# A feed-forward stage that moves its residual rows by whole groups of four batches instead of by halves

## The reference

```python
x = x + _L0_xattn_ref(_layernorm(x), ctx_1024, ctx_1024, igate_w, igate_b, fgate_w, fgate_b, out_w)
x = x + _L0_ffn_ref(_layernorm(x), L0_ffn_weight)
x = x + _L1_xattn_ref(_layernorm(x), ctx_1024, Wq, Wkv)
x = x + _L1_ffn_ref(_layernorm(x), w_gate, w_up, w_down)

def _bitlinear(x, w):
    return jnp.einsum('bsi,oi->bso', _act_quant(x), _weight_quant(w))
gate = jax.nn.silu(_bitlinear(x, w_gate))
up = _bitlinear(x, w_up)
return _bitlinear(gate * up, w_down)
```

## Time and profile before

| | us |
|---|---|
| median of three executions | 652.21 (652.16 to 652.42) |
| the profiled execution | 652.21 |
| its span, first to last instruction | 649.8 |
| PE busy | 614.1 (94%) |
| DVE busy | 567.8 (87%) |
| ACT busy | 535.9 (82%) |
| POOL busy | 454.8 (70%) |

### The profile page before, as it was taken

One profiled execution on the slowest core, in us unless ns is written; L12 is line 12 of the kernel. 1 busy time (PEld: TensorE's weight loads), 2 busy tenths in 40 slices (PEclk: granted clock), 3 DMA queues, 4 the chain that ended last, 5 costly groups with the idle time before them and its releaser, 6 DMA issues.

```text
span 649.8 us, 14695 instructions
## 1 busy us (share of the span) xinstructions
PE 614.1 (94%) x4562; PEld 456.3 (70%) x4562; DVE 567.8 (87%) x1461; ACT 535.9 (82%) x1298; POOL 454.8 (70%) x676
## 2 busy tenths in 40 slices
PE   5879999999999999999999999999899999999996
PEld 4658687687877878878787687877456556655664
DVE  4787899998898988989889889898999899999994
ACT  4577889889889789897897978965789989989985
POOL 3357586777855868658676586762677888887877
PEclk9999999999999999999999999999999999999999
DMA  8306414163351441424505233024276777686763
GB/s 291 133 8 124 98 34 131 49 146 101 80 131 50 114 106 43 131 55 111 129 18 132 58 106 99 18 66 162 46 134 163 164 167 160 157 182 158 183 124 106
DMA packets 141808, 72.53 MB, mean 112 GB/s; under 512 B 89245, under 2 KB 141470, under 8 KB 141734
## 3 DMA queue, kind: packets, MB, share of 16 engines
q1 hardware_dynamic: 134870, 68.21, 42.5%
q10 hardware_dynamic: 6864, 3.41, 1.7%
HBM read 29.39 MB, written 20.97 MB: 77 GB/s over the span
## 4 chain that ended last, share of the span: by engine, by line
PE 56%; DVE 16%; ACT 16%; issue 4%; POOL 4%; DMA 2%; SPq 1%; POOLq 0%; DVEq 0%; ACTq 0%
PE bank L743 10%; PE bank L658 8%; PE bank L711 8%; PE bank L688 8%; PE bank L762 5%; PE bank L568 4%; PE bank L732 4%; ACT ew L905 4%; PE bank L623 3%; ACT D L896 3%; DVE vg L1635 2%; DVE hmax L1642 2%; ACT x2T L872 2%; PE bank L614 2%; DVE st L1339 2%
## 5 line engine op out<-in xcount | busy, mean ns | idle before, releaser
L743 PE MATMUL bank<-WGU,fqT 128*128 128x512 bf16 x512 | 124.6, 380 | 2.4 <-DVE vg L1635 1.9
L1181 POOL TENSOR_SCALAR_AFFINE_SELECT D<-D 128x512 f32<-128x512 f32 x64 | 38.4, 635 | 85.9 <-ACT D L896 85.9
L1635 DVE SCALAR_TENSOR_TENSOR vg<-bank,back,D 128x1024 f32<-128x1024 f32 x64 | 82.0, 1280 | 7.4 <-ACT D L1076 5.8
L1076 ACT ACTIVATE D<-bank,back 128x1024 f32<-128x1024 f32 x64 | 71.4, 1115 | 18.4 <-PE bank L743 18.2
L743 PEld LDWEIGHTS bank<-WGU,fqT 128*128 128x128 bf16 x512 | 46.8, 98 | 56.4 <-DVE vg L1635 22.3
L1166 POOL TENSOR_TENSOR rs<-ve,minus_half 128x4 f32<-128x4 f32 x64 | 65.6, 1026 | 28.2 <-DVE ve L1345 26.7
L1642 DVE TENSOR_REDUCE hmax<-vg 128x1 f32<-128x1025 f32 x64 | 78.1, 1221 | 2.2
L1289 POOL TENSOR_SCALAR wtmp<-vg,hscale 128x1024 f32<-128x1024 f32 x64 | 71.6, 1119 | 5.9 <-issue 0.2
L1339 DVE BATCH_NORM_STATS2 st<-x 128x6 f32<-128x256 f32 x184 | 64.6, 413 | 2.7
L688 PEld LDWEIGHTS bank<-vaug,C 128*128 128x128 f32 x512 | 60.7, 192 | 2.2 <-issue 1.5
L658 PE MATMUL bank<-WX,qcT 128*128 128x268 f32 x256 | 62.0, 395 | 0.0
(11 more groups left out here) (200 smaller groups left out, 1537.0 us busy)
## 6 DMA issues: line engine op xcount, KB each, us to landing
xg<-in_x_dram SPq DMA_DIRECT2D x16, 512.0 KB, 3.9
cg<-in_ctx_dram SPq DMA_DIRECT2D x16, 512.0 KB, 4.6
out_dram<-x SPq DMA_DIRECT2D x15, 512.0 KB, 3.3
out_dram<-x SPq DMA_DIRECT2D x30, 256.0 KB, 2.3
xg<-out_dram SPq DMA_DIRECT2D x16, 256.0 KB, 2.9
cg<-out_dram SPq DMA_DIRECT2D x16, 256.0 KB, 3.2
rows_q<-fq ACTq DMA_DIRECT2D x13, 256.0 KB, 2.3
raw<-in_L_ffn_w_gate_dram SPq DMA_DIRECT2D x1, 1024.0 KB, 8.1
```

What stands on the lines that cost most here:

```text
L743: mm = pe.matmul(ps[k + half], fqT[:, i // 2 % 2, c, i % 2 * P:(i % 2 + 1) * P], WGU[:, c, which, half * 512:(half + 1) * 512], start=(c = ...
L1076: act.activation(fsil[:, s % 2, :], gate, ACT.Silu, scale=back[:, i, 0:1]).then_inc(g_clear, 1)
L1635: dve.scalar_tensor_tensor(out=fh[i % 2][:, 0:INNER], in0=up, scalar=back[:, i, 1:2], in1=fsil[:, i % 2, :], op0=ALU.mult, op1=ALU.mult).t ...
```

## The change

The halves go. One load of 512 KB, written inline, replaces two of 256 KB, and `half_out` becomes `group_out`: it waits for all four batches, stores them in one transfer and issues the whole load of four groups later. In the loop it moves from the even blocks (two for each group) to every fourth block, i % 4 == 3, from block 11 on. The semaphores `f_in` and `f_out` lose their second index, and POOL waits for them once in a group. Counts at the end follow.

```diff
-        f_in = [[sem(f"f_in{p}_{h}") for h in range(2)] for p in range(4)]
-        f_out = [[sem(f"f_out{p}_{h}") for h in range(2)] for p in range(2)]
+        f_in = [sem(f"f_in{p}") for p in range(4)]
+        f_out = [sem(f"f_out{p}") for p in range(2)]
...
-            def half_in(g, h):
-                some = slice(2 * h, 2 * h + 2)
-                sp.dma_start(fx[g % 4][:, some, :], grp(out, g)[:, some, :]).then_inc(f_in[g % 4][h], 16)
-
             for g in range(4):
-                for h in range(2):
-                    half_in(g, h)
+                sp.dma_start(fx[g], grp(out, g)).then_inc(f_in[g], 16)
             store(NG - 2)
-            def half_out(g, h):
-                some = slice(2 * h, 2 * h + 2)
-                sp.wait_ge(f_done, FB * g + 2 * h + 2)
-                sp.dma_start(grp(out, g)[:, some, :], fo[g % 2][:, some, :]).then_inc(f_out[g % 2][h], 16)
+            def group_out(g):
+                sp.wait_ge(f_done, FB * g + FB)
+                sp.dma_start(grp(out, g), fo[g % 2][:, :, :]).then_inc(f_out[g % 2], 16)
                 if g + 4 < NG:
-                    half_in(g + 4, h)
+                    sp.dma_start(fx[g % 4], grp(out, g + 4)).then_inc(f_in[g % 4], 16)
...
-                if i % 2 == 0 and i >= 2 * FB:
-                    half_out(i // FB - 2, i % FB // 2)
+                if i % FB == 3 and i > 2 * FB:
+                    group_out(i // FB - 2)
...
-            half_out(NG - 2, 0)
-            half_out(NG - 2, 1)
+            group_out(NG - 2)
...
-                if s % 2 == 0:
-                    pool.wait_ge(f_out[g % 2][s // 2], 8 * (g - g % 2) + 16)
-                    pool.wait_ge(f_in[g % 4][s // 2], 4 * (g - g % 4) + 16)
+                if s == 0:
+                    pool.wait_ge(f_out[g % 2], 8 * (g - g % 2) + 16)
+                    pool.wait_ge(f_in[g % 4], 4 * (g - g % 4) + 16)
```

More of the change, by code:

```diff
@@ L514, in _ @@
             for p in range(2):
-                for h in range(2):
-                    sp.wait_ge(f_out[p][h], 8 * NG + 16 - 16 * p)
+                sp.wait_ge(f_out[p], 8 * NG + 16 - 16 * p)
             sp.wait_ge(f_last, 16 * FB)
@@ L1325, in _ @@
             for p in range(2):
-                for h in range(2):
-                    dve.sem_inc(f_out[p][h], 16)
+                dve.sem_inc(f_out[p], 16)
             chain = [0]
```

## The result

| | before | changed |
|---|---|---|
| median | 653.17 us (13 runs, 651.4 to 655.8) | 657.75 us (13 runs, 655.5 to 660.5) |
| ratio | | 1.0060 (1.0042 to 1.0078) |
| profiled execution, span | 652.21, 649.8 | 658.11, 656.3 |
| third silu to last silu of the loop | 636.88 - 459.50 = 177.4 | 643.35 - 461.99 = 181.4 |
| last silu to the end of the span | 12.9 | 12.9 |

What follows compares the result with a forecast made beforehand. The prediction took the feed-forward loop's nearly full ring of TensorE, ScalarE and VectorE as the bound. Its terms, -1.1 + 0.1 + 1.45 + 0 = +0.45 us on 652.21, gave 652.7 us, with an 8 in 10 range of 651.0 to 655.7.

Steps and rivals of the forecast that it cites:

- What bounds the kernel: Feed-forward loop: TensorE, ScalarE and VectorE nearly full in a ring; the change acts through SP's transposes and at the end.
- Part 1: Odd transposes of blocks 17, 25 and 41 no longer queue behind half transfers, so their stalls go: -1.1 us.
- Part 2: Even transposes behind 1 MB, twelve blocks: margin 0.36 down to 0.06 us; 0.1 us for the nine undisturbed ones.
- T: Time at which SP issues the whole store, 2.09 us after the odd block's data is ready.
- pair of the attention loop: Transfers L403 then L407, stand-in for 512 KB after 512 KB: load lands 4.4 us after issue, 4.7 in a slower case.
- Rival B: Even transposes not held up by 1 MB; only the gain on odd ones stays: 651.1 us, chance 0.17.
- plain: Nine of the twelve even-block transposes, without a fetch or another transfer added: 0.1 us for all together.
- part 3: Even transposes of blocks 12 and 36 with a fetch, 40 with rows_q: late, together +1.45 us.
- idle of ScalarE: In each loop block ScalarE has about 0.3 us of its own idle, which swallows that much of a late transpose.
- fixed position of the fetches: 16 KB instruction fetches hang on a program position, so they hit the same loop blocks again in the changed kernel.
- Part 4: First loads, GpSimd's group waits and the kernel's end cost 0; store 13 has 0.8 us of cover before batch 60.
- Rival A: All twelve even transposes wait 0.2 to 0.3 us, some 2.7 us in all: 655.3 us, chance 0.26.

Runs made afterwards that it cites:

- changed_fourth: The changed kernel traced a fourth time, nothing altered: loop 182.1 us, ScalarE waits on us<-usq 7.5 us in 9.
- changed_third: The changed kernel traced a third time, nothing altered: loop 180.7 us, ScalarE waits on us<-usq 6.5 us in 8.
- halves_behind_odd: The kernel before with its half store and half load moved behind the odd product transposes: 0.9985, then 1.0006 when run again.
- shifted_fetches: The changed kernel with 128 semaphore increments at the very start of TensorE's program: 676.15 us (1.0338), loop 184.4 us.
- before_again: The kernel before traced a second time, nothing altered: loop 176.4 us, ScalarE waits on us<-usq 0.2 us in 1.
- before_third: The kernel before traced a third time, nothing altered: loop 177.5 us, ScalarE waits on us<-usq 1.5 us in 2.

## Why the prediction was wrong

It gave 652.7 us, +0.45, no measurable change most likely, and 0.34 to a loss; measured are +0.60%, some +4 us, which is above the top of its range, 655.7.

**What bounds the kernel** held. The change acted through the transposes on SP's queue alone; neither GpSimd's whole-group waits nor the first loads show.

**Part 1**, -1.1 us, held in kind: in no trace of the changed kernel does ScalarE wait for an odd block's transpose. In size it was lucky at best: the waits of before, 1.4 us in the trace at hand, are 0.2 in another.

**Part 2**, the position of the even transpose, was nearly right: T + 5.5 to 5.8 was worked out and T + 5.91 measured, against a need at T + 5.86 and measured T + 6.05. A margin of 0.06 to 0.36 was forecast, 0.14 found. The pair of the attention loop was a good stand-in (a load of 4.4 to 4.7 us for 4.8). The Trainium skill (DMA: Bandwidth & Descriptors, section Anatomy of one DMA) gives its fit of 2.0 us plus bytes over 436 GB/s for transfers that GpSimd issues; for these, issued by SP, each behind a store of its own size, it doesn't hold: a load of 512 KB took 4.8 us, one of 256 KB 2.9, 1.9 more and not 0.6. (By the 0.6 the load would have been in at T + 4.1 and the transpose at T + 4.6; the T + 4.7 given there for the pair doesn't follow.) Rival B, which rested beside it, did not come.

**The step that failed** is the count of the groups that something disturbs: the 0.1 us that part 2 gave to nine "plain" groups, and with it the 1.45 us of part 3, which took blocks 12, 36 and 40 for the only disturbed ones. The mechanism is right, and changed_fourth, which has the fetch set that the sum assumed, checks it block by block. Waits at the three were forecast as 0.8, 1.05 and 0.45 us before ScalarE's idle; measured 1.25, 1.24 and 1.06, together 3.55. But the same trace has six more, at blocks 20 (0.39), 24 (0.15), 32 (1.20), 44 (0.30), 48 (1.32) and 56 (0.61): 3.97 us in groups that were counted as plain. At 0.7 us of loop for each us of wait (below) that is some 2.8 us in place of 0.1, and 2.5 in place of 1.45.

Two things had been left out. The first is a 16 KB fetch ahead of the pair (blocks 31.7, 47.7 and 55.8). It was taken as over by then, but it holds up SP: the odd transpose before the pair took 2.0 to 2.4 us to issue in place of 1.19, and store, load and even transpose all went later. SP's queue in changed_fourth, blocks 47 and 48:

```profile
600.86 2.39 SPq L477 DMA_TRANSPOSE us<-usq  x1
...
604.62 1.43 SPq L477 DMA_TRANSPOSE us<-usq  x1
```

The data of the second had been ready since 603.08, 1.54 us for 0.33 in a plain group. The second is the 8 KB fetches, some ten in the loop, which end no wait where the margin is 2.5 us. In the four traces of the changed kernel, seven groups have one (and no 16 KB fetch behind it) 3.1 to 4.1 us behind the issue of the even transpose, and it landed after 5.1 to 5.3 us; a plain group's took 4.5 to 4.8, and one with a 16 KB fetch there, in eight groups, 5.8 to 6.1. In changed_fourth this is so at blocks 20, 32 and 44. Block 40 lets one compare: in changed the fetch came 4.01 us behind the issue and the wait was 1.26, in changed_third 4.35 us behind and the wait 0.66. Landing of these two:

```profile
DMA to landing us min/median/max: 5.2/5.2/5.2
```
```profile
DMA to landing us min/median/max: 4.6/4.6/4.6
```

No kernel was run that moves the 8 KB fetches. The 0.15 of block 24 stays open: its transpose landed after 4.5 us like a plain one, but was issued 0.4 us later. With 0.14 us to spare, every such event is paid.

The **idle of ScalarE** was to swallow 0.3 us of each wait. Over the traces, (181.3 - 177.1) us of loop stand against (6.95 - 1.0) us of waits, means of four and three: 0.7 us for each us of wait, which for a mean wait of 0.9 us is near the 0.3 forecast. The fixed position of the fetches, on which the prediction said it would fall, was indeed false, but the loss does not hang on it.

**Part 4** held. Store 13 went at 646.37; batch 60 is the third in GpSimd's row at 649.00, with no idle before it, and the time from the last silu to the end is the same 12.9 us. Timelines of SP and GpSimd, changed:

```profile
646.37 4.43 SPq L469 DMA_DIRECT2D out_dram<-x  x2
```
```profile
649.00 2.21 POOL L1290 TENSOR_TENSOR x<-nrm,cg 128x256 f32<-128x256 f32 x3
```

**Rival A** was the nearest: seven to nine of the twelve groups wait. It asked for a load landing over T + 5.3; it was T + 5.4. But it foresaw 0.2 to 0.3 us in every group, and what came is 0.15 to 1.95 us in the disturbed ones and none in blocks 16, 28 and 52, so even its mechanism is only half met. It had 0.26 where a loss deserved most of the chance: a margin computed at 0.06 to 0.36 us, in a stage whose rows showed delays of 1.9 us every few blocks, is no margin.

## What to carry to other kernels

Cost a merged transfer by who is served behind it, not by who waits for it: here nobody waited for the residual, and its 1 MB in one piece took the slack of a small transpose that two engines need. Large transfers were fine here when spread out: 512 KB at a time cost nothing that could be told (1.0005), the same transfers back to back 0.6%. And where a sum leaves a term a margin of tenths of a microsecond, list every disturbance in the trace, also those that end no wait today, before calling it free.

## What the hardware showed unexpectedly

- The instruction fetches of one and the same kernel fall into one of two sets of places, about 0.7 of a block apart with a long gap elsewhere; halves_behind_odd had one in its first trace (7.3, 12.3, 20.4, ...) and the other in its second (7.9, 13.3, 18.4, ...). What chooses is open.
- 128 semaphore increments on TensorE ran from 4.2 to 23.6 us in shifted_fetches, 0.15 us each.
- A single 8 KB instruction fetch in the right place moved a transpose's landing by about 0.6 us, one of 16 KB by about 1.4 us (4.5 to 4.8 us without, 5.1 to 5.3 and 5.8 to 6.1 with).
- Equal kernels differ by 2 to 4 us before the loop: before_again has its first silu at 454.8 us, before_third at 457.2, changed_third at 454.6, changed_fourth at 458.8. The granted clock tells them apart. From 33.5 to 40.3 us it was 0.50 (1.2 GHz) in before_third and 1.00 (2.4 GHz) in before_again; from 20 to 33 us TensorE had been busy for 10.78 us in both. PEclk of the two pages, before_again and before_third:

```profile
PEclk9999999999999999999999999999999999999999
```
```profile
PEclk9979999999999999999999999999999999999999
```

So a loss or gain of 1 us is better read from the loop's own rows than from the span. What lowers the clock there wasn't looked into.
